# Six middle images of a fused convolution-attention and attention block: an engine loop replaced by written-out code with constant waits

## What is computed

```
x = x + neighbourhood_attention(group_norm(x))     # 16 heads of 8, 7x7 window, position bias, projection
t = tokens of x                                    # 3136 x 128
t = t + attention(layer_norm(t))                   # 8 heads of 16, all 3136 x 3136 scores, softmax
t = t + (layer_norm(t) @ dequant(qidx, scales).T) @ W.T
```

## Time and profile before

| | |
|---|---|
| median of three runs | 9278.91 us |
| the profiled execution, its time | 9294.23 us |
| its span, first to last instruction | 9292.4 us |
| mean granted TensorE clock | 0.981 of full speed |
| TensorE matmuls busy | 8644.9 us, 93% |
| VectorE, ScalarE, GpSimd busy | 79%, 73%, 31% |
| front of image 0 alone | 0 to 498.18 us |
| image 0 | 498.18 to 1602.86 us |
| images 1 to 6 (the loop) | 1602.86 to 8423.71 us |
| image 7 and the last tail | 8423.71 to 9292.4 us |

### The profile page before, as it was taken

How to read it: one execution, slowest core, us unless ns; L and a number is a source line. 1 busy time by engine, 2 the same in 40 slices (tenths; PEclk the granted TensorE clock), 3 DMA queues, 4 the chain that set the end, 5 groups by cost and what they waited for, 6 DMA issues and landing times.

```text
span 9292.4 us, 432513 instructions
## 1 busy us (share of the span) xinstructions
PE 8644.9 (93%) x173512; PEld 4571.7 (49%) x173512; DVE 7385.2 (79%) x12442; ACT 6737.1 (73%) x14241; POOL 2839.5 (31%) x2805
## 2 busy tenths in 40 slices
PE   5789999999999999999999999999999999999998
PEld 4445554555445554455544555545545455444443
DVE  5577878888788887878878887788877888788985
ACT  2367777777777777777777777777777777778877
POOL 5514441244302443034430343304433044320000
PEclk8899999999999999999999999999999999999999
DMA  1120101101011010110101100020011201011000
GB/s 44 35 53 20 26 22 41 30 20 26 25 42 26 21 28 24 43 27 18 28 24 49 24 19 25 24 55 17 22 27 27 45 17 25 25 28 30 9 10 9
DMA packets 312339, 257.30 MB, mean 28 GB/s; under 512 B 97244, under 2 KB 303052, under 8 KB 308300
## 3 DMA queue, kind: packets, MB, share of 16 engines
q1 hardware_dynamic: 310348, 229.05, 10.1%
HBM read 136.82 MB, written 78.05 MB: 23 GB/s over the span
## 4 chain that ended last, share of the span: by engine, by line
PE 84%; issue 6%; DVE 4%; ACT 3%; POOL 2%; DMA 1%; SPq 0%; ACTq 0%; DVEq 0%; POOLq 0%
PE PS L1240 22%; PE PS L1172 22%; PE PS L1225 20%; PE PS L978 6%; PE PS L1036 5%; PE PS L1044 4%; PE PS L1054 2%; DVE block_max L1704 1%; ACT PB L1456 1%; PE PS L1028 1%; ACT tail L1374 1%; PE PS L1084 0%; PE PS L1010 0%; DVE NM L1581 0%; DMA vT_padded<-SC 0%
## 5 line engine op out<-in xcount | busy, mean ns | idle before, releaser
L1704 DVE TENSOR_REDUCE block_max<-PS 128x1 f32<-128x512 f32 (+1 forms) x9632 | 6134.7, 683 | 1214.7 <-PE PS L1172 1139.3
L1456 ACT ACTIVATE PB<-PS 128x448 f32<-128x448 f32 (+1 forms) x11200 | 5459.0, 545 | 1599.3 <-PE PS L1225 1573.7
L1225 PE MATMUL PS<-QP,KP 99*32 99x448 bf16 x43904 | 4320.5, 355 | 82.6 <-ACT PB L1456 52.3
L1172 PE MATMUL PS<-KP,QP 96*32 96x512 bf16 (+1 forms) x43904 | 4011.9, 356 | 91.5 <-issue 79.9
L1240 PE MATMUL PS<-PB,VA 128*32 128x448 f32 x22400 | 2720.7, 541 | 26.4 <-issue 25.8
L1225 PEld LDWEIGHTS PS<-QP,KP 99*32 99x32 bf16 x43904 | 1415.1, 97 | 1290.0 <-issue 466.6
L1172 PEld LDWEIGHTS PS<-KP,QP 96*32 96x32 bf16 x43904 | 1283.3, 96 | 1507.4 <-issue 587.8
L1240 PEld LDWEIGHTS PS<-PB,VA 128*32 128x32 f32 x22400 | 787.1, 111 | 421.4 <-issue 51.9
L884 POOL TENSOR_TENSOR SC<-SC,NM 128x1120 f32<-128x1120 f32 x210 | 433.1, 2063 | 1826.7 <-DVE NM L1581 1826.6
L858 POOL TENSOR_TENSOR QB<-Qn,C 128x896 f32<-128x896 f32 x392 | 662.0, 1709 | 12.0 <-ACT Qn L1314 12.0
L1036 PE MATMUL PS<-KR,QB 128*32 128x80 f32 x21952 | 553.7, 234 | 82.3 <-DVE VS L1620 22.2
(11 more groups left out here) (114 smaller groups left out, 4717.6 us busy)
## 6 DMA issues: line engine op xcount, KB each, us to landing
QP<-q_dram SPq DMA_DIRECT2D x672, 56.0 KB, 2.1
VP<-vT_padded SPq DMA_DIRECT2D x448, 70.0 KB
k_dram<-k_parts SPq DMA_DIRECT2D x56, 336.0 KB, 2.9
KP<-k_dram SPq DMA_DIRECT2D x336, 56.0 KB, 2.1
q_dram<-q_parts SPq DMA_DIRECT2D x56, 336.0 KB, 2.5
KP<-k_dram SPq DMA_DIRECT2D x48, 392.0 KB, 6.4
VA<-v_dram SPq DMA_DIRECT2D x16, 816.0 KB, 4.3
vT_padded<-SC SPq DMA_DIRECT2D x112, 112.0 KB
```

What stands on the lines that cost most here:

```text
L1172: ins = mm(PS[at:at + QT, bank, n * width:(n + 1) * width], QP[0:ROWS, Q_SLOTS[k % AUNITS], t:t + QT], KP[0:ROWS, g, t // BLK, keys], star ...
L1225: ins = mm(PS[k0:k0 + 32, bank, 0:BLK], KP[0:ROWSM, k // NBLK, h, c * P + k0:c * P + k0 + 32], QP[0:ROWSM, Q_SLOTS[k], h * BLK:(h + 1) * B ...
L1456: S.activation(exp_buffer(k, c)[0:n, h, :], PS[0:n, at % ST_BANKS, 0:BLK], ACT.Exp, scale=float(ADIM) ** -0.5).then_inc(exp_done, 1)
L1704: V.tensor_reduce(block_max[:, k % 2, queries.start:queries.stop, j], tile, AX.X, ALU.max).then_inc(max_read, 1)
```

## The change

Images 1 to 6 are written out by a Python loop, with b as a plain number. `wait` skips waits for values that are not positive, as before for plain numbers. `apart`, its semaphore and all its calls go, in the front and in all images. Where `apart` stood between two waits or behind a last wait, the waits now stand directly before the next instruction. No matmul, activation, reduction or transfer changes, nor does the order of tasks.

```diff
         def wait(eng, s, value):
 
-            if not isinstance(value, int) or value > 0:
+            if value > 0:
                 eng.wait_ge(s, value)
-
-        def apart(eng):
-
-            eng.sem_inc(paced, 1)
...
-            return t[b + ahead:b + ahead + 1] if isinstance(b, int) else t[bass.ds(b + ahead, 1)]
+            return t[b + ahead:b + ahead + 1]
...
-        def each_image(eng, image):
+        def each_image(image):
 
             image(0, "first")
-            if images > 2:
-                with eng.Fori(1, images - 1) as b:
-                    image(b, "middle")
+            for b in range(1, images - 1):
+                image(b, "middle")
             image(images - 1, "last")
             image(images, "after")
...
                 def scores(s, p, bank):
                     pe.wait_ge(queries_in, of(b, ahead, STRIPS, s + 1))
                     pe.wait_ge(keys_rolled, of(b, ahead, STRIPS, s + 1))
-                    apart(pe)
...
                 def turn(s, c, bank):
                     pe.wait_ge(normalised, of(b, ahead, STRIPS, s + 1))
-                    apart(pe)
...
                 def values(s, bank):
                     pe.wait_ge(turned_read, of(b, ahead, 4 * STRIPS, 4 * s + 4))
                     pe.wait_ge(windows_in[s % 2], of(b, ahead, 16 * windows_loaded(STRIPS - 2 + s % 2), 16 * windows_loaded(s)))
-                    apart(pe)
...
                         pe.wait_ge(*side_read(b, 1, *previous[0]))
-                        apart(pe)
                         do(*plan.taken[t, sub], SIDE_BANK)
...
                     wait(pe, exp_done, of(b, 0, AUNITS * GH * CHUNKS, k * (GH * CHUNKS) + at + 1 - ST_BANKS + seam))
-                    if n < P:
-                        apart(pe)
```

More of the change, by code:

```diff
@@ L442, in hybrid_block @@
         early_in, weights_in = sem("early_in"), sem("weights_in")
-        paced = sem("paced")
         table_filled, table_cols_in = sem("table_filled"), sem("table_cols_in")
@@ L602, in arrived @@
                 wait(sp, s, value)
-                if not isinstance(value, int):
-                    apart(sp)
             def load(dst, src):
@@ L800, in image @@
                             do(task, i)
-            each_image(sp, image)
+            each_image(image)
             sp.wait_ge(y_out, images * (16 * NBLK))
@@ L827, in roll_keys @@
                     wait(pool, scores_in, of(b, ahead, 3 * STRIPS, 3 * s))
-                    apart(pool)
                     k_img = Kn.rearrange("p o (y x) -> p (o y) x", x=SIDE)
@@ L964, in image @@
                             do(task, i)
-            each_image(pool, image)
+            each_image(image)
         @block.tensor
@@ L1280, in image @@
                         maxima(len(steps))
-            each_image(pe, image)
+            each_image(image)
         @block.scalar
@@ L1295, in gn_var @@
                     act.wait_ge(gn_in, of(b, ahead, 2, 2))
-                    apart(act)
                     S.activation(gn[:, 7:8], PS[:, bank, 0:1], ACT.Ln, bias=eps5).then_inc(gn_log, 1)
@@ L1463, in image @@
                                 beside(k * CHUNKS + c, 1)
-            each_image(act, image)
+            each_image(image)
         @block.vector
@@ L1532, in gn_sums @@
                     dve.wait_ge(stats_in, of(b, ahead, NBLK, NBLK))
-                    apart(dve)
                     V.bn_aggr(gn[:, 0:2], stats[:, :, :]).then_inc(gn_cols, 1)
@@ L1752, in image @@
                             take_max(b, later, m)
-            each_image(dve, image)
+            each_image(image)
 def kernel(x, L0_conv_qkv_w, L0_conv_rpb, L0_conv_proj_w, L0_conv_proj_b, L1_attn_Wq, L1_attn_bq, L1_attn_Wk,
```

## The result

The changed kernel takes 8967.03 us, the median of four runs (8956.54 to 8970.16); the kernel before took 9279.86 beside it. The ratio is 0.9663, with a 95% interval of 0.9651 to 0.9675: 313 us or 3.4% faster.

What follows compares the result with a forecast made beforehand. TensorE, busy 93% of the span, was taken as the bound. Savings of 50.9 + 10.4 + 92.4 + 16 = 169.7 us gave 9124.5 us profiled, 9110 us by the median (1.8% faster), range 9060 to 9190.

Steps and rivals of the forecast that it cites:

- the term for `apart`: Removing `apart` calls everywhere: 2 us an image, 14 us in seven, plus 2.3 in the front; together 16 us saved.
- 110 us: Upper bound for `apart` on TensorE outside `beside`: 308 calls an image, 15.7 us of sequencer time, in seven images.
- The rival "more is exposed": Half of the 110 us of TensorE's `apart` time lies bare, 39 us more saved: about 9070 us; chance 0.12.
- The seam: Last unit of images 1 to 5, which branch back: written out there is no taken branch, saving 50.9 us.
- The slow clock behind it: First 48 matmuls after a branch back run at 0.51 of full clock: five times 2.09, 10.4 us saved.
- Units 1 to 12 of the loop form: Six loop images against image 0: register instructions and fetch stalls cost 107.4 us, of which 92.4 come back.
- the allowance of 15 us: Two long fetch stalls at 7.5 us in units 1 to 12, assumed to remain in the written-out images.
- the three terms: Loop form's savings: last units 50.9 us, slow clock after branches 10.4, units 1 to 12 of six images 92.4.
- The rival of the seam alone: Image 0's units 1 to 12 are quicker for another reason; only 61.3 us come back, 9218 us; chance 0.12.
- The rival of a worse straight stream: Written-out code stalls more in fetch after `values` bursts; at 1.3 us more a strip 9328 us; chance 0.03.
- The counts: Expected in the new profile: about 1,375 instruction packets, not 1,457; TensorE semaphore instructions from 660 to about 350 an image.

Runs made afterwards that it cites:

- the two written-out kernels: Images 1 to 6 written out by a Python loop: with all calls of `apart` kept 9141.55 us, without them (the changed kernel) 8967.03 us.
- the kernel of three loops: Kernel before with three loops of two turns in place of one of six, register instructions and `apart` kept: 9253.42 us, ratio 0.9964.
- four kernels: Looped ones: kernel before (9279.86 us), three loops of two turns (9253.42), and kernel before with 128 (9281.80) or 64 (9388.12) TensorE increments ahead of image 0.
- the two kernels with `apart` and constants: Kernel before with middle images written out (9141.55 us), or each in a one-turn loop whose wait values became constants when compiled (9132.44 us).
- the shift: 64 semaphore increments on TensorE ahead of image 0, here added to the changed kernel: 8961.29 us, ratio 0.9652.
- the one with loops of one turn and constants: Kernel before with each middle image in its own one-turn loop, `apart` kept; wait values became constants when compiled: 9132.44 us, ratio 0.9852.

## Why the prediction was wrong, and where it was right

**The step that failed** is the term for `apart`: "I take 4% of it, 0.6, and in full the 28 in `values`", 16 us together. Measured: 174.5 us between the two written-out kernels by their medians, 20.1 us in image 0 alone (1102.17 to 1082.06 in the profiled executions). Three things in it were wrong.
- The calls in `beside` were left out, because they "carry a wait that must stay in some instruction". They are 352 in image 3, more than the 308 that were priced. Without them that wait sits on the weight load, which has to be issued anyway. They alone cost 101 us, the largest part.
- The other calls were spread evenly over TensorE's time, and only the open share of it was taken. They are not spread evenly: in a task of `beside` they stand right behind the wait for the reader of the side bank, where the array runs out of work in the place shown above. TensorE's calls together cost 153 us and those in `beside` 101, so the others cost some 52 us where 16 were forecast. Of 43 us without work in image 0, 25 are left.
- The calls of the other engines were taken at nothing. They cost 14 us by themselves, 21 on top of TensorE's.

Each call was also priced at its own 51 ns, though increments in a row start 0.15 us apart. So 110 us was no true bound from above for the 308 calls an image. It isn't what failed: these calls came to 52 us, since most of their time stayed hidden.

The rival "more is exposed" had the right mechanism and about the right size, half of 110 us, for the calls that it was about. It left out `beside` too, and so stayed at 9070 us.

**The seam**, 50.9 us forecast for the last units: 50.4. The slow clock behind it, 10.4: the first units of images 2 to 6 are 10.9 us shorter in the profile after; that of image 1, which no branch back precedes, is 2.8 us shorter. The gap is gone.

**Units 1 to 12 of the loop form**, 92.4 us forecast: 82.7 with `apart` kept. Image 0 was a fair model of them, as it has constants and no loop, though without the allowance of 15 us it would have given 107.4. By the medians the whole loop form came to 134 us, 19 less than the 153.7 of the three terms, which hides a little of what the term for `apart` lacked. The rival of the seam alone (9218) falls. (Six turns of the loop written out are six times its code, not 13 times; no term rests on this.)

**What this term is made of** is only partly settled. In the kernel of three loops the loop form costs 15 us an image. The 24 looped images of four kernels, in six places of the code, take 993.94 us or more for these units; the 12 of the two kernels with `apart` and constants take 989.69 or less. The register instructions are the plain difference, but no run has them without a loop. The `values` chunk of the earlier trace rows takes 3.10 us in the changed kernel, as in image 0. But the lie of the stream moved a loop by up to 122 us, so part of the 83 us may be that of the kernel before. I had called it chance and given it no width of its own. That the gaps are TensorE's instruction fetch is my reading of their place behind bursts of small products and of their moving with the shift; no run took the fetch away. Long stalls beside other transfers I can't price apart either.

**The rival of a worse straight stream** fell: 8961 and 8967 us with and without the shift. Here it was the loop that was exposed to a bad lie.

**The counts.** Instruction packets 1,375 forecast, 1,367 found. TensorE's semaphore instructions: about 350 an image forecast, 380 found in image 3. 112 of them are at the wait of `turn`, 84 in `scores` and 28 at the line of `wait`.

Images of 1100 to 1115 us were forecast, 1085 to 1090 came.

## What to carry to other kernels

Ask of each sequencer instruction which wait it stands behind. In this kernel one behind the wait that is satisfied last cost 40 ns on the mean, and two of them delayed a weight load by 0.22 us in the place looked at; an engine's busy share of 95% did not hide them. Ahead of that wait the same instruction cost nothing that could be measured. A wait that must stay does not need the instruction that carries it: it can sit on the next real one. Code of the new form that the old trace already holds (here the first image) was a good model, but only for what differs between the two: what the change takes from both must be priced by itself. The looped kernel took from 9282 to 9388 us by where its code lay; shift such a loop by some instructions before ascribing a per cent to anything.

## What the runs showed of the hardware that was not expected

- 64 increments ahead of a loop, run once, cost 102 us of 9286 (1.1%). With 128 the time was the same as with none: 20 us lost in units 1 to 12, 32 gained in the last units, some lost elsewhere. The same 64 ahead of the written-out code cost nothing.
- Semaphore increments in a row on TensorE, each recorded with 51 ns, start 0.15 us apart (64 of them in 9.7 us).
- A taken branch back on TensorE made the last unit 10.1 us longer on the mean in one lie and 3.7 us in another.
- One semaphore instruction of 51 ns on TensorE cost 40 ns on the mean behind the wait for the side bank's reader, and nothing measurable ahead of it (5 us over 2,521, within the noise).
- ScalarE was busy 5074.10 us in the six looped images and 5001.84 in the six written out with `apart`, with the same number of activations. It goes with the waits from registers: in units 1 to 12 the kernel of three loops has 4457.64 us, the one with loops of one turn and constants 4399.15. No run here shows why.
